# Moving the first loads and the first convolution of a kernel's last stage into the stage before it

## The reference, cut to what matters

```python
x = x + attn(cond(x, cond_128, ...), ...)    # stages 1 and 2
x = x + ffn(cond2(x, cond_128, ...), ...)    # stage 3

# attn: a Mamba-like layer with 8 groups
proj = einsum('bld,pd->blp', hidden, in_proj_w)       # gate, x, B, C, dt
conv = conv_bias + sum(pad[:, k:k+L] * conv_weight[:, k])  # 4 taps, then silu
...                                                    # scan, gated RMS norm, out_proj

# cond2: grouped convolution along the 512 columns, 9 taps, 4 groups, plus a context
out = conv_general_dilated(x, weight, padding=[(4, 4)], feature_group_count=4)
out = out + ctx[:, :, None] + bias[None, :, None]

# ffn: one of two weight matrices for each token, by the norm of its row
mask = norm(x) > 64
y = where(mask, x @ w_h.T, x @ w_l.T) + bias           # w_h: 8-bit codes, w_l: 4-bit codes
```

## Time and profile before

| | |
|---|---|
| median of 3 runs | 3618.82 us (3617.97 to 3620.92) |
| the profiled execution's own time | 3620.42 us |
| its span in the profile | 3618.7 us |
| PE busy | 3519.7 us, 97% of the span |
| DVE busy | 3082.9 us, 85% |
| ACT busy | 1459.2 us, 40% |
| POOL busy | 468.5 us, 13% |
| DMA | 490.29 MB, mean 135 GB/s |

### The profile page before, as it was taken

How to read it: one execution, slowest core, us unless ns; L and a number is a source line. 1 busy time by engine, 2 the same in 40 slices (tenths; PEclk the granted TensorE clock), 3 DMA queues, 4 the chain that set the end, 5 groups by cost and what they waited for, 6 DMA issues and landing times. The chain is left out here.

```text
span 3618.7 us, 58730 instructions
## 1 busy us (share of the span) xinstructions
PE 3519.7 (97%) x19789; PEld 2875.8 (79%) x19789; DVE 3082.9 (85%) x4879; ACT 1459.2 (40%) x2218; POOL 468.5 (13%) x298
## 2 busy tenths in 40 slices
PE   6699999999999999999999999999999999997999
PEld 4488888888888888888888888888888888886888
DVE  6599999999999999999999999999999999997343
ACT  3444444444444344444344444444444434442111
POOL 3100111100111100111110011110011111001333
PEclk9799999999999999999999999999999999998999
DMA  7623244323533343324433353334332452334331
GB/s 247 244 99 128 102 163 164 116 110 128 191 111 128 125 175 135 123 98 167 168 111 116 128 186 116 128 118 176 141 114 106 164 172 110 116 127 119 103 92 56
DMA packets 220672, 490.29 MB, mean 135 GB/s; under 512 B 39594, under 2 KB 85066, under 8 KB 211042
## 3 DMA queue, kind: packets, MB, share of 16 engines
q1 hardware_dynamic: 216388, 488.86, 38.5%
q0 software_dynamic: 304, 0.82, 0.1%
q10 hardware_dynamic: 3952, 0.27, 0.1%
HBM read 320.51 MB, written 169.39 MB: 135 GB/s over the span
## 5 line engine op out<-in xcount | busy, mean ns | idle before, releaser
L790 PE MATMUL bank<-ht,wt 128*128 128x512 f32 x7680 | 1862.4, 397 | 8.0 <-DMA ht<-h_d 8.0
L790 PEld LDWEIGHTS bank<-ht,wt 128*128 128x128 f32 x7680 | 1425.6, 188 | 354.4 <-issue 19.2
L1012 DVE SCALAR_TENSOR_TENSOR xc<-bank,cvw,xc 128x496 f32<-128x496 f32 (+2 forms) x1152 | 820.7, 717 | 96.7 <-ACT xc L927 45.8
L927 ACT ACTIVATE xc<-bank,cvb,cvw 128x512 f32<-128x512 f32 x384 | 299.7, 781 | 1128.1 <-PE bank L790 1128.1
L885 PE MATMUL bank<-wot,gy 128*128 128x512 f32 x3072 | 738.2, 396 | 0.0
L885 PEld LDWEIGHTS bank<-wot,gy 128*128 128x128 f32 x3072 | 567.3, 188 | 128.3 <-issue 11.0
L766 POOL TENSOR_TENSOR r<-rv,neg_half 128x4 f32<-128x4 f32 x64 | 90.5, 1413 | 2490.7 <-DVE rv L1100 2490.7
L1034 DVE TENSOR_TENSOR m<-cbm,y 128x1024 f32<-128x1024 f32 x256 | 301.5, 1219 | 7.8
L763 POOL TENSOR_TENSOR segr<-adts,mask_le 128x1024 fp32r<-128x1024 f32 x128 | 242.8, 1919 | 377.9 <-DVE adts L1003 377.9
L917 ACT ACTIVATE gy<-z 128x512 fp32r<-128x512 f32 x256 | 162.1, 633 | 320.5 <-DVE z L1074 320.5
L913 ACT ACTIVATE z<-bank 128x512 f32<-128x512 f32 x256 | 150.5, 588 | 278.7 <-PE bank L790 278.7
(11 more groups left out here) (166 smaller groups left out, 3048.0 us busy)
## 6 DMA issues: line engine op xcount, KB each, us to landing
ht<-h_d SPq DMA_DIRECT2D x64, 2048.0 KB, 7.9
acc<-acc_d SPq DMA_DIRECT2D x64, 1024.0 KB, 7.2
wt_d<-wnext SPq DMA_DIRECT2D x128, 512.0 KB, 3.1
acc_d<-acc SPq DMA_DIRECT2D x64, 1024.0 KB, 4.3
wt<-wt_d SPq DMA_DIRECT2D x70, 512.0 KB, 8.4
stage<-in_L_attn_in_proj_w SPq DMA_DIRECT2D x106, 256.0 KB, 2.8
h_d<-ht_out SPq DMA_DIRECT2D x8, 2048.0 KB, 8.2
wot<-wt_d SPq DMA_DIRECT2D x28, 512.0 KB, 6.3
```

What stands on the lines that cost most here:

```text
L790: ins = pe.matmul(pb[:, :], wt[:, n, l, k, :], ht[:, rr, k, :], start=(q == 0 and k == 0), stop=(q == 2 and k == KC - 1))
L927: act.activation(xc[:, n, :], bank[PROJ_BANK[n]][:, :], ACT.Identity, bias=cvb[:, n:n + 1], scale=cvw[:, n, TAPS - 1:TAPS]).then_inc(s_tap, 1)
L1012: ins = dve.scalar_tensor_tensor(dst, src, cvw[:, n, TAPS - 1 - k:TAPS - k], dst, ALU.mult, ALU.add)
```

## The change

Stage 3's first data moves forward, and so does the first convolution.

- `wt`, `ht` and `acc` of stage 2 get fixed addresses at the top of the on-chip memory. The places of `wt` and `ht` are used again, still in the last pass, for `w4_nat`, `x2p0`, `x2_0`, `ctx_all` and `bias`.
- In the last pass SP loads `w4_nat`, the eight pieces of `x2p0` and `x2_0` after the seventh projection, and `ctx_all` and `bias` after the tenth.
- The raw convolution weights are loaded in stage 1, behind the first loads of `x`. POOL spreads them at the start of stage 2 (36 products), where DVE did so in stage 3.
- PE convolves tiles 0 and 1 at the end of stage 2, into the two banks `p_cv` that all stages now share.
- The wait for the last store of `acc` goes from the end of stage 2 to SP's program in stage 3, behind the loads of block 1.
- In stage 3 the 4-bit weights are turned first, the turned weights lie in other banks, and ACT and DVE split them in two halves of four with the first tile's work in between. ACT's loop begins one tile later.

```diff
@@ stage 1, SP, behind load_x
+                w_v = a["L0_cond2_weight"].rearrange("(q o) i k -> q i o k", o=CG)
+                for s in range(R):
+                    for q in range(L // CG):
+                        lo = s * L + q * CG
+                        sp.dma_start(sh.cbn[lo:lo + CG, :, :], w_v[q]).then_inc(sh.s_cbn, 16)
@@ stage 2, SP, step(): over is true in the last pass
+                    if over:
+                        sp.wait_ge(s_proj, NPJ * it + 7)
+                        sp.dma_start(sh.w4_nat[:, :, :].rearrange("p t i -> p (t i)"), sh.w4_d).then_inc(sh.s_w, 16)
...
+                                sp.dma_start(sh.x2p0[s * L:(s + 1) * L, bs, 1:1 + P], x2p_v[0, s, :, bs, :]).then_inc(sh.s_x2p[0][h], 16)
+                        sp.dma_start(sh.x2_0[:, :, :, :].rearrange("p t r m -> p t (r m)"), acc_v[0]).then_inc(sh.s_x2[0], 16)
                     sp.wait_ge(s_nlo, 2 * it + 2)
...
                     sp.wait_ge(s_proj, NPJ * (it + 1))
                     if not over:
                         load_h((j + 1) % NBLK)
+                    else:
+                        sp.dma_start(sh.ctx_all[:, :], sh.ctxb_d.rearrange("b o -> (b o)").partition_broadcast(P)).then_inc(sh.s_par, 16)
+                        sp.dma_start(sh.bias[:, :], a["L0_ffn_bias"].partition_broadcast(P)).then_inc(sh.s_par, 16)
...
-                sp.wait_ge(s_accst, 16 * NIT + 16)
                 sp.wait_ge(s_nst, 32 * NIT + 32)
@@ stage 2, POOL, ahead of its loop
+                pool.memset(sh.cbq[:, :, :, :], 0.0).then_inc(sh.s_mask, 1)
...
+                pool.wait_ge(sh.s_cbn, 16 * R * (L // CG))
...
+                                pool.tensor_tensor(sh.cbq[rows, q, r_out, :].rearrange("p (g o) -> p g o", o=CG),
+                                                   sh.cbn[rows, :, k].unsqueeze(1).to_broadcast([L, L // CG, CG]), same,
+                                                   ALU.mult).then_inc(sh.s_cbq, 1)
@@ behind POOL's loop
+                pool.memset(sh.x2p0[:, :, 0:1], 0.0).then_inc(sh.s_halo, 1)
+                pool.memset(sh.x2p0[:, :, 1 + P:], 0.0).then_inc(sh.s_halo, 1)
@@ stage 2, PE, behind its loops
+                pe.wait_ge(s_z, CT * NIT + CT)
+                pe.wait_ge(s_nlo, 2 * NIT)
+                pe.wait_ge(sh.s_cbq, NCBQ)
+                pe.wait_ge(sh.s_halo, 2)
+                pe.wait_ge(sh.s_x2p[0][0], 16 * R)
+                for t in range(2):
+                    conv2(pe, bank[t], sh.x2p0, sh.cbq, t).then_inc(sh.s_cv, 1)
@@ stage 3
-        p_tr = p_y[0] + p_y[1]
+        p_tr = p_y[1] + p_ss + p_y[1] + [p_ss[1], p_y[0][1]]
+        READ_OUT = (0, 0, 0, 0, 1, 2, 4, 0)
...
                 load_phases(0, 1)
                 load_rows(0, 1)
+                sp.wait_ge(sh.s_accst, 16 * NIT + 16)
...
-                for q, w in ((1, sh.w8), (0, w4)):
+                pe.wait_ge(s_w, 16)
+                for w in (w4, sh.w8):
                     for r in range(R):
-                        if n >= 4:
-                            pe.wait_ge(s_wlo, n - 3)
+                        if READ_OUT[n]:
+                            pe.wait_ge(s_wlo, READ_OUT[n])
...
+                weights_high(0)
+                tile(0, 0)
+                weights_high(1)
...
                 context(0, 0, 0)
+                weights_low(0)
+                context(0, 0, 1)
                 norm(0, 0, 0)
-                context(0, 0, 1)
+                weights_low(1)
                 norm(0, 0, 1)
@@ build(): fixed places, in bytes above TOP = 163808
+        sh.wt = at_top("wt", [P, NCV + CT, 2, KC, P], 0, F32R)
+        sh.ht = at_top("ht", [P, 2, KC, BLK], WT_BYTES, F32R)
+        sh.acc = at_top("acc", [P, TT, DM], WT_BYTES + HT_BYTES)
+        sh.w4_nat = at_top("w4_nat", [P, OT, DM], W4_AT)
+        sh.x2p0 = at_top("x2p0", [P, BLK // L, MW], X2P_AT)
+        sh.x2_0 = at_top("x2_0", [P, TT, R, P], X2_AT)
+        sh.ctx_all = at_top("ctx_all", [P, TOK], CTX_AT)
+        sh.bias = at_top("bias", [P, DM], BIAS_AT)
```

More of the change, by code:

```diff
@@ L65 @@
 NCV = 2 + CT
+NPJ_ALL = NCV + CT
 NWC = NCV + CT + KC
@@ L757, in _ @@
                 pool.sem_inc(s_segr, 2)
+                pool.memset(sh.cbq[:, :, :, :], 0.0).then_inc(sh.s_mask, 1)
+                pool.memset(sh.gmask[:, :], 1.0).then_inc(sh.s_mask, 1)
+                v = sh.gmask[:, :].rearrange("p (q o) -> p q o", o=CG)
+                for n, (base, step, cm) in enumerate(((0, -CG, 1), (CG - 1, CG, -1))):
+                    pool.wait_ge(sh.s_mask, n + 2)
+                    pool.affine_select(out=v, in_=v, compare_op=ALU.is_ge, fill=0.0, base=base,
+                                       pattern=[[step, P // CG], [0, CG]], channel_multiplier=cm).then_inc(sh.s_mask, 1)
+                pool.wait_ge(sh.s_cbn, 16 * R * (L // CG))
+                pool.wait_ge(sh.s_mask, 4)
+                for s in range(R):
+                    rows = slice(s * L, (s + 1) * L)
+                    same = sh.gmask[rows, rows].rearrange("p (g o) -> p g o", o=CG)
+                    for q in range(NQ):
+                        for r_out in range(R):
+                            k = R * q + s - r_out
+                            if 0 <= k < KW:
+                                pool.tensor_tensor(sh.cbq[rows, q, r_out, :].rearrange("p (g o) -> p g o", o=CG),
+                                                   sh.cbn[rows, :, k].unsqueeze(1).to_broadcast([L, L // CG, CG]), same,
+                                                   ALU.mult).then_inc(sh.s_cbq, 1)
+                pool.wait_ge(sh.s_cbq, NCBQ)
                 with pool.Fori(0, NIT) as it:
@@ L1113, in _, with conv2 @@
                                                          ALU.mult, ALU.add).then_inc(s_acc, 1)
+def conv2(pe, out, phases, cbq, t):
+    for b in range(BT):
+        for q in range(NQ):
+            ins = pe.matmul(out[:, b * P:(b + 1) * P], phases[:, BT * t + b, q:q + P], cbq[:, q, :, :].rearrange("p r o -> p (r o)"),
+                            start=(q == 0), stop=(q == NQ - 1))
+    return ins
 def stage3(nc, a, sh, out):
@@ L1123, in sem @@
             return ctx.enter_context(nc.semaphore(name))
-        w4 = sb("w4_nat", [P, OT, DM])
+        w4, ctxb, bias, cbq = sh.w4_nat, sh.ctx_all, sh.bias, sh.cbq
         wq = sb("wq", [P, 2, 2, R, DM], F32R)
[L1127 to L1133, removed]
+        x2 = [sh.x2_0, sb("x2_1", [P, TT, R, P])]
+        x2p = [sh.x2p0, sb("x2p1", [P, BLK // L, MW])]
         xb = sb("x2b", [P, TT, DM])
@@ L1293, in conv @@
                     pe.wait_ge(s_x3, no(jj, u, t) + 1)
-                    for b in range(BT):
-                        for q in range(NQ):
-                            ins = pe.matmul(p_cv[t % 2][:, b * P:(b + 1) * P], x2p[u][:, BT * t + b, q:q + P],
-                                            cbq[:, q, :, :].rearrange("p r o -> p (r o)"),
-                                            start=(q == 0), stop=(q == NQ - 1))
-                    ins.then_inc(s_cv, 1)
+                    conv2(pe, p_cv[t % 2], x2p[u], cbq, t).then_inc(s_cv, 1)
                 def squares(jj, u, t):
```

139 lines of the change are left out of this document (58 added, 81 removed).

## The result

The changed kernel takes 3560.57 us (median; the other runs lie between 3558.48 and 3564.81), the kernel before 3618.90 us beside it: a ratio of 0.984 with an interval of 0.9823 to 0.9857. That is 58 us less. The forecast was 3598.9 us, 20 less, in a range from 3595.5 to 3604.0: wrong, since the gain is nearly three times as large.

What follows compares the result with a forecast made beforehand. PE, busy 97% of the span, was taken as the bound; a shorter step from stage 2 to 3 brings its second product 19.9 us earlier, 3618.82 - 19.9 = 3598.9 us, range 3595.5 to 3604.0.

Steps and rivals of the forecast that it cites:

- What is added and should be hidden: Added loads, POOL's 36 products and moved tiles, in all stages: hidden behind other work or free, no cost.
- The forecast's first sentence: Whole kernel: PE is at 97% of the span, so gains are work taken off PE or less standing still.
- the moved tiles cost each pass: Rival, stage 2's 64 passes: slower reads at new addresses, 0.31 us a pass cancels the gain, 0.62 gives 3638.6; chance 0.03.
- The end of stage 2: Stage 2's end: convolution of 5.7 us replaces SP's 3.9 us wait, PE comes last, block's end 2.2 us earlier.
- The start of stage 3: Stage 3's start: 5.9 us from first transpose to first product, through turned weights and DVE; other four low parts hidden.
- The allowance of 1.3 us for slow transposes: Stage 3's start: if transposes are slow already, 3.63 us for 16, the gain is 1.3 us less.
- The clock: Stage 3's first product: PE's clock falls during the transposes, so the first period again costs 10.06 us.
- the warm rival: Rival, stage 3's start: the clock stays up, second product at 3334.5, 21.4 us gained, 3597.4 us; chance 0.26.
- work in front: Rival, start of stage 2: POOL at 1.41 us a product makes PE wait 5.9 us, 3604.8 us; chance 0.07.
- Late code: Rival, behind the loops and the block's end: PE waits 2.2 us for a code fetch, 3601.1 us; chance 0.12.
- The period in stage 3: Stage 3's loop from the second product on: stays at 8.52 us a tile, so everything behind moves as one piece.

Runs made afterwards that it cites:

- place_only: The kernel before with only wt, ht and acc at the changed kernel's fixed addresses, no work moved: 3584.33 us, ratio 0.9905.
- wt_lower: The changed kernel with wt alone 192 bytes lower: 3593.34 us, ratio 0.9928.
- wait_kept: The changed kernel with the wait for the last store back at the end of stage 2: 3564.25 us, ratio 0.9845.
- work_only: The changed kernel with all moved work, but stage 2's tiles at the addresses of the kernel before: 3596.44 us, ratio 0.9940.
- micro1: A separate kernel of products alone, 24 for each of 157 address pairs: 233.3 ns at before's wt and ht addresses, 226.7 at the changed ones.
- micro2: A separate kernel of product series, with eight offsets of either operand in steps of 32 bytes and others: 226.7 ns at distance 0, 228.9 at 64.

## Why the prediction was wrong

- **The step that failed** is the last sentence of "What is added and should be hidden": "Moving wt, ht and acc costs nothing in any row: products from `wt` and `wot` run alike." It was a term put at nothing, and it was minus 0.52 us in each pass, minus 34 in all. The forecast's first sentence had left no room for it: it knew two gains, less work on PE or less standing still, and not the same products at a shorter spacing. `place_only` has that gain without the work, `wt_lower` loses it with the work in place, and the two series give the cause, the distance of the operands modulo 256 bytes.
- The sentence also leaned on the wrong row. The 12 products of the earlier trace rows from `wt` last 2.95 and 3.07 us, those from `wot` 3.01: single rows of twelve, whose ends are modelled. A mean over a steady stretch was to be had in the same trace: 16.79 us for 72 starts, 233 ns each, against 229 for the output products. "Run alike" was false by 4 ns, and the prediction doesn't ask where they come from.
- The rival "the moved tiles cost each pass" had the right place and the right size to look for (0.31 us a pass cancel the gain) and only one sign. It was not bounded below nothing: a mirror of 0.31 us would have put the range's lower end at 3579, still 18 us above the measured time.
- **The end of stage 2** held: 5.52 us of convolution (5.7 foreseen), first transpose 5.83 us behind the last product's end (6.44 foreseen), idle 0.48 us before it. As forecast, the block's end is set by PE and no longer by SP.
- **The start of stage 3** held: 5.81 us to the first product (5.9 foreseen), the second half of the weights hidden. The allowance of 1.3 us for slow transposes doesn't follow from the earlier trace rows, where 16 take 3.63 us and not 2.08 and only four stand on the path, 0.4 us; `wait_kept`, where they were slow, lost 0.33.
- **The clock**: the rival was right, it stayed up. The first product took 5.75 us, the period to the second 8.41. The step became 22.2 us shorter; the forecast had 19.9, the rival 21.4. The 2.35 us by which the forecast's sum was short are 1.65 of the clock, 0.6 of the earlier first transpose and 0.1 behind it. `work_only`, at 3596.44, is where the warm rival put the changed kernel (3597.4).
- **What is added**: POOL's 36 products took 8.33 us, 0.23 each, hidden; no load was late. The rival "work in front" didn't come. SP's 16 loads in front took 12.69 us and not 7.7 and still ended at 17.4, before 20.62. The moved bytes add up to 6.55 MB, not 6.3, which shifts their end by 1 us and changes nothing. The first product with `segr` came at 192.69 in place of 189.32 in the changed kernel's profile, with the late first rows of that execution, and at 188.3 to 191.1 in the other kernels with the same loads in front.
- **Late code** wasn't seen: PE's idle time before its first transpose is 0.48 us, and the 2.2 us of a fetch have no room in it; at the other new place, behind the loops, the convolution began 0.16 us before the modelled end of the last product. The rule of the Trainium skill (Runtime: NRT & Kernel Launch, Instruction fetch mechanics) had no price here that a run shows.
- The period in stage 3 was taken as unchanged; it fell from 8.52 to 8.41 us, 3.5 us in all, with the spacing (234 to 229 ns): 24 products of 5 ns are 0.12 us.

## What to carry to other kernels

Before a tile is moved, compute for each dense series of products the distance of its two operands modulo 256 bytes, before and after (shown here for products of 128x128 by 128x512 in float32r). A gap of 64 bytes was worth 1.2% of this kernel, more than all the work moved at the step. Where a change lays out memory anew, its gain is to be split by a kernel that has the addresses alone and one that has the work alone, or the work gets praise that belongs to the addresses. And a row of the timeline is too coarse for a per cent: for a product's price take the distance of starts over a stretch without waits.

## What the runs showed of the hardware

- A product of 128x128 by 128x512 in float32r takes 226.7 ns start to start where its operands lie a multiple of 256 bytes apart, 228.9 at a remainder of 64, and 231.7 to 234.6 at the other multiples of 32, at the full clock, with all other engines idle (`micro1` and `micro2`). Where in the memory they lie made a difference only at a remainder of 128 (231.7 to 233.3). Why the distance counts isn't shown by any run.
- A small DVE operation can last as long as a POOL operation beside it. In the changed kernel's profiled execution the scaling of 8 columns lasted 3.86 us, where it had taken 0.28, and PE's next product waited for it, to 17.25 us in place of 13.48. DVE and POOL in the same stretch, and then DVE in `wait_kept`, which has the same stage 1:

```profile
13.34 3.86 DVE L454 TENSOR_SCALAR att<-att,erec 128x8 f32<-128x8 f32 x1
```
```profile
13.38 3.78 POOL L287 COPY xp<-xb 128x2048 f32<-128x2048 f32 x1
```
```profile
12.72 0.36 DVE L454 TENSOR_SCALAR att<-att,erec 128x8 f32<-128x8 f32 x1
```

  The Trainium skill (SBUF — State Buffer, SBUF: two separate sides) describes the ports that the two share as an exclusive lock that the one which starts first gets for its whole instruction. The rows agree in part: the two end within 0.04 us of each other, but by its row the scaling, which was held, began 0.04 us before the copy; and no row shows whether a scaling of this kind takes the shared ports. In every other kernel here it began at 12.4 to 13.1 us, ahead of the copy by 0.2 us or more, and took 0.23 to 0.37. So it befell one of the twelve profiled executions (those of `micro1` and `micro2` have no such work), and the moved loads alone don't bring it about.
- The 16 small loads in front took SP 12.69 us to issue, 0.79 each. In stage 3 of the kernel before loads of the same shape took 0.48 each (eight in 3.87 us), and SP's single loads take 0.42 to 0.45. Why they are slower in front isn't shown.

```profile
4.75 12.69 SPq L208 DMA_DIRECT2D cbn<-in_L_cond_weight  x16
```
